# Dynamic convolution kernel: new order of work on ScalarE, VectorE and TensorE around the statistics of the next sample

## The reference, cut to what matters

```
x: (16, 256, 56, 56) f32; weight: (4, 256, 256, 3, 3); att_w: (4, 256); att_b: (4)

g      = group_norm(x, 32 groups, eps 1e-5)
pooled = mean(g, axis=(2, 3))                       # per sample and channel
att    = sigmoid(pooled @ att_w.T + att_b)          # (16, 4)
agg_w  = einsum('nk,kocij->nocij', att, weight)     # a 3x3 kernel of its own for each sample
out    = x + conv3x3(g[n], agg_w[n], padding 1)     # for each n
```

## Time and profile before

| | us |
|---|---|
| median of 3 runs | 1508.08 (1504.42 to 1510.9) |
| the profiled execution | 1502.79 |
| its span | 1501.2 |
| TensorE busy | 1327.3 (88%) |
| VectorE busy | 1193.4 (79%) |
| ScalarE busy | 919.4 (61%) |
| mean granted TensorE clock | 0.961 |

### The profile page before, as it was taken

How to read it: one execution, slowest core, us unless ns; L and a number is a source line. 1 busy time by engine, 2 the same in 40 slices (tenths; PEclk the granted TensorE clock), 3 DMA queues, 4 the chain that set the end, 5 groups by cost and what they waited for, 6 DMA issues and landing times.

```text
span 1501.2 us, 25281 instructions
## 1 busy us (share of the span) xinstructions
PE 1327.3 (88%) x8808; PEld 739.8 (49%) x8808; DVE 1193.4 (79%) x2000; ACT 919.4 (61%) x1466; POOL 59.0 (4%) x77
## 2 busy tenths in 40 slices
PE   0269989899898989989898998989899898989995
PEld 0135545455454545545454554545455454545552
DVE  3998878879787887978788797878879787887961
ACT  6567665766765676676567667556666656666420
POOL 0000000000000000000000000000000000000000
PEclk9989999999999999999999999999999999999998
DMA  8011534444143444424354442434434243443334
GB/s 341 16 70 41 132 86 130 130 124 124 49 130 94 129 130 104 127 63 127 100 131 130 98 125 60 130 108 129 130 73 128 77 129 113 130 129 69 84 87 107
DMA packets 29373, 165.70 MB, mean 110 GB/s; under 512 B 3360, under 2 KB 3616, under 8 KB 28192
## 3 DMA queue, kind: packets, MB, share of 16 engines
q0 software_dynamic: 9216, 51.38, 20.2%
q1 hardware_dynamic: 20000, 112.34, 20.2%
HBM read 112.33 MB, written 51.38 MB: 109 GB/s over the span
## 4 chain that ended last, share of the span: by engine, by line
PE 52%; DVE 17%; DMA 12%; issue 12%; ACT 4%; DVEq 0%; SPq 0%; ACTq 0%; POOL 0%; POOLq 0%
PE pM L399 46%; DMA X<-x_dram 12%; PE pG L374 6%; DVE Us L543 3%; DVE E L533 3%; DVE T L492 2%; DVE X L620 2%; DVE T L527 2%; DVE X L608 1%; ACT G L823 1%; DVE E L518 1%; DVE W L743 1%; DVE Vs L549 1%; ACT Us L794 1%; ACT unused L842 1%
## 5 line engine op out<-in xcount | busy, mean ns | idle before, releaser
L399 PE MATMUL pM<-Vs,Us 128*128 128x392 f16 x6912 | 1216.8, 338 | 93.9 <-ACT TB L804 74.7
L399 PEld LDWEIGHTS pM<-Vs,Us 128*128 128x128 f16 x6912 | 679.3, 100 | 620.2 <-ACT TB L804 80.6
L549 DVE TENSOR_TENSOR Vs<-E,Vs 128x784 f16<-128x784 f32 x192 | 185.2, 972 | 90.9 <-ACT Vs L784 90.9
L784 ACT CAST Vs<-E 128x784 f16<-128x784 f32 x192 | 159.9, 845 | 87.2 <-DVE E L518 56.0
L492 DVE SCALAR_TENSOR_TENSOR T<-X 128x392 f32<-128x392 f32 x384 | 194.1, 561 | 2.3 <-ACT X L829 0.2
L794 ACT CAST Us<-E 128x768 f16<-128x768 f32 x128 | 103.1, 829 | 122.7 <-DVE E L533 122.7
L842 ACT ACTIVATE unused<-X 128x784 bf16<-128x784 f32 x128 | 109.5, 856 | 80.5 <-DMA X<-x_dram 72.3
L812 ACT ACTIVATE X<-pM,small 128x392 f32<-128x392 f32 x128 | 73.0, 584 | 103.0 <-PE pM L399 103.0
L374 PE MATMUL pG<-W,D 128*32 128x512 f16 x1728 | 104.8, 388 | 32.1 <-DVE W L743 32.1
L829 ACT ACTIVATE X<-X,small 128x1568 f32<-128x1568 f32 x64 | 107.8, 1689 | 35.7 <-DVE small L583 35.7
L850 ACT ACTIVATE unused<-X,small 128x784 bf16<-128x784 f32 x128 | 121.4, 948 | 6.3
(11 more groups left out here) (72 smaller groups left out, 542.0 us busy)
## 6 DMA issues: line engine op xcount, KB each, us to landing
X<-x_dram SPq DMA_DIRECT2D x64, 784.0 KB, 5.4
X<-x_dram POOLq DMA_DIRECT2D x64, 784.0 KB, 8.0
out_dram<-X SPq DMA_DIRECT2D x64, 784.0 KB, 3.8
W<-w_dram SPq DMA_DIRECT2D x6, 1152.0 KB, 17.2
X<-w_dram SPq DMA_DIRECT2D x2, 1152.0 KB, 25.4
attw<-attw_dram SPq DMA_DIRECT2D x1, 128.0 KB, 8.5
small<-attb_dram SPq DMA_DIRECT2D x1, 0.5 KB, 9.2
```

The lines of the kernel that those rows point to most:

```text
L399: mm = pe.matmul(tile_rows(bank(k, o)), Us[:, j, a, c, o, kx, :], v_in(j, b, c, kx), start=(at < 2 and n == 0), stop=(n == 3 * KS * CT - 1 ...
L549: dve.tensor_tensor(v_out(v[2], 1), e_planes(("V", *v)), v_out(v[2], 0), ALU.subtract).then_inc(v_lo, 1)
L784: act.copy(v_out(j, 0), e_planes(("V", *v))).then_inc(v_hi, 1)
```

## The change

No instruction is added or taken away: the lists of TensorE, VectorE and ScalarE are put into another order, and the tables follow. On ScalarE both passes `sums` of chunk 1 move behind `take_first(1, 1)` and the four `take_pair` of chunk 0. On TensorE the mean matmul moves behind group (5, 1), the variance matmul behind (6, 0), the logits behind (7, 0), and the three mixes behind (8, 0), (8, 1) and (9, 1). On VectorE the V items of points 3 and 4 of the next sample come ahead of the U items, V of points 0 and 5 of chunk 0 is made an epoch earlier, and `add_rows(9, 1)` comes behind `take_edge(11, 1)`. The lists that run once before the loop get the same order.

```diff
 ACT_TAKES = [
-    (0, 0), (1, 0), (0, 1), (2, 0), (1, 1), (3, 0), (2, 1), (3, 1),
+    (0, 0), (0, 1), (1, 0), (1, 1), (2, 0), (2, 1), (3, 0), (3, 1),
...
             # TensorE
                 group(e, 4, 1)
+                group(e, 5, 0)
+                group(e, 5, 1)
                 if more:
                     group_mean_mm(e)
-                group(e, 5, 0)
+                group(e, 6, 0)
                 if more:
                     group_var_mm(e)
-                group(e, 5, 1)
-                group(e, 6, 0)
-                if more:
-                    logits_mm(e)
                 group(e, 6, 1)
                 group(e, 7, 0)
                 if more:
+                    logits_mm(e)
+                group(e, 7, 1)
+                group(e, 8, 0)
+                if more:
                     mix(e, 0)
-                group(e, 7, 1)
+                group(e, 8, 1)
                 if more:
                     mix(e, 1)
-                group(e, 8, 0)
-                group(e, 8, 1)
-                if more:
-                    mix(e, 2)
                 group(e, 9, 0)
                 group(e, 9, 1)
+                if more:
+                    mix(e, 2)
...
             # ScalarE, first part of the epoch
-                take_pair(e, b, 2, 0)
-                v_high(e, (0, 0, 0))
-                if more:
-                    sums(e, 1 - b, 1, 0)
-                take_first(e, 1, 1)
-                take_pair(e, b, 3, 0)
-                take_pair(e, b, 2, 1)
-                v_high(e, (0, 1, 3))
-                if more:
-                    sums(e, 1 - b, 1, 1)
+                take_first(e, 1, 1)
+                take_pair(e, b, 2, 0)
+                v_high(e, (0, 1, 1))
+                u_high(e, (0, 1, 5))
+                v_high(e, (0, 0, 5))
+                take_pair(e, b, 2, 1)
+                v_high(e, (0, 1, 2))
+                take_pair(e, b, 3, 0)
+                take_pair(e, b, 3, 1)
+                if more:
+                    sums(e, 1 - b, 1, 0)
+                    sums(e, 1 - b, 1, 1)
+                v_high(e, (0, 1, 3))
+                v_high(e, (0, 1, 0))
+                v_high(e, (0, 1, 4))
+                if more:
+                    root(e)
...
             # VectorE, end of the epoch
-                add_rows(e, b, 9, 0)
-                take_edge(e, b, 11, 0)
-                take_edge(e, b, 10, 0)
-                take_edge(e, b, 10, 1)
-                if more:
-                    v_pair(e, 1 - b, ("V", 1, 0, 3))
-                    u_low(e, (1, 1, 3))
-                    v_low(e, (1, 0, 3))
-                add_rows(e, b, 9, 1)
-                take_edge(e, b, 11, 1)
+                take_edge(e, b, 11, 0)
+                take_edge(e, b, 10, 1)
+                if more:
+                    u_pair(e, ("U", 1, 1, 3))
+                    u_low(e, (1, 1, 3))
+                take_edge(e, b, 11, 1)
+                if more:
+                    u_low(e, (1, 0, 0))
+                add_rows(e, b, 9, 1)
+                if more:
+                    v_single(e, 1 - b, ("V", 1, 0, 0))
+                    u_low(e, (1, 1, 2))
+                    v_single(e, 1 - b, ("V", 1, 0, 5))
```

More of the change, by code:

```diff
@@ L427, in epoch @@
                 if more:
+                    logits_mm(e)
+                group(e, 7, 1)
+                group(e, 8, 0)
+                if more:
                     mix(e, 0)
-                group(e, 7, 1)
+                group(e, 8, 1)
                 if more:
                     mix(e, 1)
-                group(e, 8, 0)
-                group(e, 8, 1)
+                group(e, 9, 0)
+                group(e, 9, 1)
                 if more:
                     mix(e, 2)
-                group(e, 9, 0)
-                group(e, 9, 1)
                 group(e, 10, 0)
@@ L639, in epoch @@
-                v_low(e, (0, 1, 3))
-                take_other(e, 2, 1)
-                take_other(e, 3, 0)
+                v_pair(e, b, ("V", 0, 1, 1))
+                take_other(e, 2, 0)
+                u_low(e, (0, 1, 0))
+                u_low(e, (0, 1, 5))
+                v_low(e, (0, 0, 0))
+                u_low(e, (0, 0, 5))
+                take_other(e, 3, 0)
+                take_other(e, 2, 1)
+                v_single(e, b, ("V", 0, 1, 5))
+                v_low(e, (0, 1, 2))
@@ L642, in epoch @@
+                add_rows(e, b, 3, 0)
+                take_other(e, 3, 1)
+                v_low(e, (0, 1, 1))
+                v_low(e, (0, 0, 5))
+                take_edge(e, b, 4, 0)
+                v_pair(e, b, ("V", 0, 1, 3))
                 if more:
                     channel_stats(e)
-                v_pair(e, b, ("V", 0, 1, 1))
+                take_edge(e, b, 4, 1)
+                v_single(e, b, ("V", 0, 1, 0))
                 if more:
                     group_shift(e)
-                take_other(e, 3, 1)
@@ L648, in epoch @@
-                take_edge(e, b, 4, 1)
+                take_edge(e, b, 5, 0)
+                v_low(e, (0, 1, 3))
                 if more:
                     group_variance(e)
-                v_low(e, (0, 1, 1))
-                take_edge(e, b, 4, 0)
+                v_low(e, (0, 1, 4))
                 if more:
                     norm_scale(e)
[L655 to L658, removed]
+                v_low(e, (0, 1, 5))
@@ L659, in epoch @@
+                take_edge(e, b, 5, 1)
+                add_rows(e, b, 3, 1)
+                v_low(e, (0, 1, 0))
                 if more:
                     attention(e)
-                add_rows(e, b, 3, 1)
-                take_edge(e, b, 5, 1)
-                v_low(e, (0, 1, 0))
+                    v_pair(e, 1 - b, ("V", 1, 0, 1))
+                    v_pair(e, 1 - b, ("V", 1, 0, 3))
+                    v_low(e, (1, 0, 3))
+                    v_low(e, (1, 0, 1))
+                take_other(e, 8, 1)
@@ L673, in epoch @@
                     u_pair(e, ("U", 1, 0, 3))
                     u_low(e, (1, 0, 2))
-                take_other(e, 8, 0)
-                take_other(e, 9, 0)
-                take_other(e, 8, 1)
-                if more:
+                    u_low(e, (1, 0, 1))
                     u_pair(e, ("U", 1, 1, 1))
                 take_other(e, 9, 1)
+                take_edge(e, b, 10, 0)
                 if more:
+                    u_low(e, (1, 1, 1))
                     u_low(e, (1, 0, 3))
+                add_rows(e, b, 9, 0)
@@ L747, in _ @@
             v_pair(0, 0, ("V", 1, 0, 1))
-            u_pair(0, ("U", 1, 0, 1))
-            u_low(0, (1, 0, 1))
+            v_pair(0, 0, ("V", 1, 0, 3))
+            v_low(0, (1, 0, 3))
             v_low(0, (1, 0, 1))
             v_low(0, (1, 0, 2))
+            u_pair(0, ("U", 1, 0, 1))
+            v_low(0, (1, 0, 4))
             u_pair(0, ("U", 1, 0, 3))
             u_low(0, (1, 0, 2))
+            u_low(0, (1, 0, 1))
             u_pair(0, ("U", 1, 1, 1))
+            u_low(0, (1, 1, 1))
             u_low(0, (1, 0, 3))
             u_low(0, (1, 0, 4))
-            u_low(0, (1, 1, 1))
+            u_pair(0, ("U", 1, 1, 3))
+            u_low(0, (1, 1, 3))
+            u_low(0, (1, 0, 0))
+            v_single(0, 0, ("V", 1, 0, 0))
             u_low(0, (1, 1, 2))
[L759 to L762, removed]
+            v_single(0, 0, ("V", 1, 0, 5))
             first[0] = steps[0]
@@ L902, in epoch @@
                     norm(e, 1 - b, 0, 1)
-                v_high(e, (0, 1, 5))
-                v_high(e, (0, 1, 2))
+                    norm(e, 1 - b, 1, 1)
+                    norm(e, 1 - b, 1, 0)
+                    exponential(e)
+                    norm(e, 1 - b, 0, 0)
                 take_first(e, 7, 0)
+                take_first(e, 7, 1)
+                take_first(e, 6, 1)
                 if more:
@@ L908, in epoch @@
                     take_taps(e, 1)
+                take_pair(e, b, 8, 0)
+                if more:
                     take_taps(e, 2)
-                take_first(e, 6, 1)
+                    v_high(e, (1, 0, 3))
+                    v_high(e, (1, 0, 1))
+                    v_high(e, (1, 0, 2))
+                    take_taps(e, 3)
+                take_pair(e, b, 8, 1)
                 if more:
-                    take_taps(e, 3)
                     take_taps(e, 4)
-                    v_high(e, (1, 0, 1))
-                    u_high(e, (1, 0, 1))
-                take_first(e, 7, 1)
+                take_pair(e, b, 9, 0)
                 if more:
                     take_taps(e, 5)
-                take_pair(e, b, 8, 0)
-                if more:
-                    v_high(e, (1, 0, 2))
+                    v_high(e, (1, 0, 4))
+                    take_taps(e, 6)
                     u_high(e, (1, 0, 2))
[L923 to L926, removed]
                     take_taps(e, 7)
-                    u_high(e, (1, 0, 3))
+                    u_high(e, (1, 0, 1))
                     take_taps(e, 8)
@@ L960, in _ @@
                 take_taps(0, m)
```

(4 more changed lines are left out.)

79 lines of the change are left out of this document (28 added, 51 removed), and 6 rows, old and new, of the table E_ITEMS.

## The result

The changed kernel takes **1405.56 us** (median), the kernel before 1506.25 in the same comparison: a ratio of 0.9329, 95% interval 0.9288 to 0.9369, so 6.7% faster. That median is over four runs, one of which was disturbed (1985.97 us at a granted clock of 0.663) and is left out of the ratio; the other three lie between 1404.19 and 1406.64, with a median of 1404.48. The profiled execution took 1404.19, its span is 1402.6.

What follows compares the result with a forecast made beforehand. TensorE's wait for ScalarE's TB copy, itself behind a load, plus slow clock was taken as the cost: 102.8 us over 14 epochs and 1.4 at the start off 1502.79, plus 3.4, gave 1402 us; range up to 1430.

Steps and rivals of the forecast that it cites:

- forecast case: Whole kernel: the change works as planned, 1402 us, by itself 1394 to 1412; chance 0.70.
- The sum: Whole kernel: 14 epochs x (88.04 - 80.7) = 102.8 us, plus 1.4 at the start: 104 us less, 1398.6 profiled.
- the 3.4 us that I added for the median: Offset from profiled execution to median: runs lay 1.6 to 8.1 us above it, part expected to go with the load's wait.
- (a): ScalarE: chunk 1's `sums` leave the way of TB's copy; TensorE's wait of 4.6 to 5.3 us and slow clock go.
- The epoch: Loop epoch: 88.04 us on average falls to 80.7; 80.39 without the loop gap, which stays in one epoch of two.
- the three losses that I took off the old epoch: TensorE in an 88.41 us epoch: 4.60 us idle, 2.82 of slow clock, 0.60 at the loop's return.
- (b): Chunk 1's loads land at 23.6 and near 27 us, ScalarE reaches the passes at 25.1; margins 1.5 and some 2.
- (c): Chain from sums to mix: later, but TensorE asks later too; margins 1.9, 1.7 and 2.2 us.
- (d): VectorE from mix to next epoch: tightest places have 1.1 to 1.8 us; loop return of 1.35 fits a 1.8 wait.
- rival 1: A margin is overrun: 1 us of new wait an epoch gives 1416 us, 3 us gives 1464; chance 0.14.
- (e): Lists before the loop: TensorE starts some 3 us later, but a 3.00 us wait and its slow clock go; 1.4 gained.
- Rivals 2 to 5: Loads late, 1416 us (0.03); VectorE bounds, 1473 (0.07); wait moves to mean matmul, 1500 to 1510 (0.02); slower, 1560 (0.04).

Runs made afterwards that it cites:

- e2: Changed kernel with `sums(1, 0)` alone put back ahead of `take_first(1, 1)` on ScalarE: 1532.97 us, ratio 1.0168.
- e3: Kernel before, only SyncE's queue reordered to store o = 0, load c = 0, store o = 1, load c = 1: 1424.9 us, ratio 0.9451.
- e4_seam_moved: Changed kernel with VectorE's loop return moved behind the low part of V (0, 5), some 29.5 us into an epoch: 1393.84 us, ratio 0.9245.
- e8: Changed kernel with VectorE's loop return moved ahead of `v_single` (0, 1, 5), some 23 us into an epoch, beside two plain loads: 1415.24 us, ratio 0.9359.
- e1_sums_only: Kernel before, only ScalarE's `sums(1, 0)` moved behind `take_first(1, 1)`, `take_pair(3, 0)` and `take_pair(2, 1)`: 1460.79 us, ratio 0.9689.

## Why the prediction was right

1402 was forecast, 1405.56 measured (1404.48 over the undisturbed runs), in the forecast case's own range (1394 to 1412).

**The mechanism was right, the closeness partly luck.** The sum gave 1398.6 for the profiled execution, which took 1404.19: 5.6 too little, 5.1 of it in the epochs. Two errors of opposite sign stand in those: 0.4 us too much in each epoch without waits, and 1.1 us an epoch for the loop returns and what follows from them, where 0.3 was put. Then the 3.4 us that I added for the median, taken from runs 1.6 to 8.1 above the profiled one, closed more than half of that without a cause: the median of the undisturbed runs lies 0.3 above the profiled one.

- **(a) The wait and its clock go.** Shown: no wait for TB, clock 0.988 instead of 0.961. The waits that went were 4.60 to 6.81 us, not 4.6 to 5.3, and the slow clock behind them cost 1.3 to 2.9 us (rows of 54 matmuls from 10.58 to 12.16 us against 9.28), so the 2.82 that I read was nearly the dearest. The mechanism is shown from both sides, by putting the pass back (e2) and by bringing the load earlier (e3).
- **The epoch.** Forecast 80.7, measured 81.06. The epoch without waits is 79.98, not 80.39. I took a group at 3.06 us, the row of seven with its modelled end; from start to start it is 3.04 (48.58 us for 16 groups). So each of the three losses that I took off the old epoch came out 0.07 to 0.17 us too small.
- **(b) The load's place.** Right in the end, by two errors that cancel. I had the adds 1.2 and 8.8 us into the epoch; they were issued at 745.17 and 752.42 with the epoch begun at 745.37, so at -0.2 and 7.1. And I had the load land 14.8 us after the second add; in e2, where ScalarE stood waiting for it, it was 16.7 (724.00 to 740.74). In the changed kernel the data of both loads had ended by 770, and ScalarE began the passes 25.0 us into the epoch, where I had 25.1. No epoch waited.

```profile
769.00:770.00 1.00, 1.00 (x7) 0.58 (x6) 1.00 (x3) 0.36 (x2) 0.00 (x0) 1.00 0.14 57
770.00:771.00 1.00, 1.00 (x7) 0.59 (x6) 1.00 (x3) 1.00 (x2) 0.00 (x0) 1.00 0.00 0
770.35 0.84 ACT L848 ACTIVATE unused<-X 128x784 bf16<-128x784 f32 x1
```

- **(c), (d) The margins.** In the loop TensorE waited for none of the mean, the variance, the logits or the mix. V (0, 5) at group (5, 0), named as the tightest place with 1.1 us, was the one that was overrun (but for 0.17 us at group (4, 0), once), and only in epochs with VectorE's loop return. The step that was mis-sized is the return: I took its 1.35 us over from the earlier trace rows and put it under a cover of 1.8; it was 3.75 to 5.61, now that the new lists bring VectorE to it while an add moves. It cost 0.66 to 1.94 us of waiting in five of the six epochs that have it, none where the gap was 3.75, and TensorE's return 0.63 to 0.97 where I had 0.60. That is a small new wait (rival 1) in five epochs of fifteen, 7.5 us in all.
- **(e) The start.** TensorE's first group stands at 94.55 (forecast some 3 us after 91.45, measured 3.1), and no gap follows. Counting from the mean matmul, two groups or 6.1 us later in the new list, the start gained 128.17 - (133.63 - 6.1) = 0.6 us, not 1.4. The gap of 3.00 went with the slow clock behind it, but the slow clock behind the long wait for the first group stayed, and lasted longer: at a granted clock of 0.50 and 0.58 TensorE started 22 matmuls in its first 6 us, where it was 28 before (0.50 and 0.89).
- **Rivals 2 to 5** didn't come: the adds are 7.25 us apart at 745.17 and 752.42, and 7.0 to 8.3 over the span, where they were 7.0 to 8.4 before; VectorE's waits outside the return come to 5.6 and 6.7 us in the two epochs shown above. So the rule of the Trainium skill (SBUF — State Buffer, "SBUF: two separate sides") that the prediction held against the change, a DMA of GpSimd's queue held up while VectorE holds the shared port, has nothing to show here, with VectorE busier than before, 85% against 79%; that VectorE's operations of this kernel hold that port at all wasn't tried.

## What to carry to other kernels

An engine that runs a fixed list pays for a transfer at the place where the list asks for it, and so do all that stand behind it: look up what the other engines need next, and put the instruction that waits for a transfer behind it, or bring the transfer earlier in its queue. Here the new lists gave 101 us, the earlier load alone 83, both together no more than the lists. One call of `sums` moved alone gave 47, since the next waits in the list take its place. When a list is shortened to the bound of one engine, the loop's return becomes visible: try it at another place, away from transfers first (here 12 us), and write the bounding engine's list out (5 more).

## What the runs showed that I had not expected

- The gap at VectorE's loop return changes with its place and goes with the data under way: 3.75 to 5.61 us beside an add (DMA share in the gap 0.66 and more), 2.49 to 3.99 beside two loads or just at their end, 1.13 to 1.37 just behind an add (0.00 to 0.19), none in e4_seam_moved (0.01). Both lists show short and long gaps, so the list isn't the cause; why 1.2 us are left at one place without data and nothing at another is open.
- The waits of TensorE in the loop up to 1.84 us that are shown here left the granted clock alone (9.28 us for 54 matmuls behind 1.60). Between 2.1 and 2.5 us both came: 2.21 in e8 and 2.40 and 2.48 in e1_sums_only left it alone, 2.16 in e8 (a granted clock of 0.72 behind it) and 2.47 in e1 didn't. One of 2.67 us didn't either: in e1_sums_only 18 matmuls behind it took 4.66 us at a granted clock of 0.64, instead of 3.06.

```profile
722.02:726.68 4.66, 4.66 (x18) 2.48 (x19) 2.56 (x10) 3.05 (x7) 0.00 (x0) 0.64 0.00 0
```

- One call of `sums` moved in the old lists gave 47 us, and the same call put back in the new ones lost 127: the size of a step says little about its share, since the lists only work together.
